# Eight-head attention: four heads scored together on 32-row tiles, with a second, transposed scoring in place of transposes

## The reference

```python
# L2; hidden is (2, 128, 16, 16), S = 256 places, HEADS = 8 of 16 channels
qk_hs = concat([hidden, embedding], axis=1)         # 128 + 64 channels; the embedding is constant
q, k, v = qk_hs @ Wq, qk_hs @ Wk, hidden @ Wv       # per place; split into 8 heads of 16
scores = einsum('bhqd,bhkd->bhqk', q, k) * 16 ** -0.5
attn = softmax(scores, axis=-1)
o = einsum('bhqk,bhkd->bhqd', attn, v)              # heads side by side: 128 channels
x3 = (o @ Wout + bout) + hidden                     # input of block L3
# L3 begins: f = chan_ln(x3) * g; q, k, v = dwconv3x3(conv1x1(f)); ...
```

## Time and profile before

| | |
|---|---|
| runs | 93.95, 95.25, 97.65 us; median 95.25 |
| profiled execution: span from the first to the last instruction | 94.5 us, 1637 instructions |
| what lies around the span | not recorded for that execution; median of the runs less the span is 0.75 us |
| granted TensorE clock | 1.000 over the span |
| busy: PE / weight loads / DVE / ACT / POOL | 84.6 / 61.4 / 67.1 / 53.2 / 30.9 us |
| DMA | 5.01 MB, 53 GB/s over the span |

### The profile page before, as it was taken

One profiled execution on the slowest core, in us unless ns is written; L12 is line 12 of the kernel. 1 busy time (PEld: TensorE's weight loads), 2 busy tenths in 40 slices (PEclk: granted clock), 3 DMA queues, 4 the chain that ended last, 5 costly groups with the idle time before them and its releaser, 6 DMA issues.

```text
span 94.5 us, 1637 instructions
## 1 busy us (share of the span) xinstructions
PE 84.6 (90%) x510; PEld 61.4 (65%) x510; DVE 67.1 (71%) x195; ACT 53.2 (56%) x168; POOL 30.9 (33%) x62
## 2 busy tenths in 40 slices
PE   4987999999999789899999999899999868979960
PEld 1333789756776569588776766678899635756540
DVE  1527456684677675997778699697999983877861
ACT  3200035924942504899989996996199454903830
POOL 7006199200000009910010003048876840235320
PEclk9999999999999999999999999999999999999999
DMA  1899100000000000772930000000000000000003
GB/s 52 228 363 390 44 0 0 0 0 7 0 0 3 0 0 0 237 210 68 285 98 0 0 0 0 0 7 0 0 0 3 0 0 10 0 0 3 0 0 111
DMA packets 5561, 5.01 MB, mean 53 GB/s; under 512 B 304, under 2 KB 5040, under 8 KB 5552
## 3 DMA queue, kind: packets, MB, share of 16 engines
q1 hardware_dynamic: 5264, 4.18, 13.4%
q10 hardware_dynamic: 288, 0.72, 2.6%
HBM read 3.59 MB, written 1.31 MB: 52 GB/s over the span
## 4 chain that ended last, share of the span: by engine, by line
PE 51%; DVE 19%; ACT 9%; issue 6%; POOL 6%; DMA 5%; SPq 0%; POOLq 0%; DVEq 0%; ACTq 0%
PE bank L886 7%; PE bank L1067 6%; DMA wa<-in_pack_a 5%; POOL vacc L277 3%; PE bank L1086 3%; ACT p L400 3%; DVE st L506 3%; PE bank L879 3%; PE bank L909 2%; DVE nmax L700 2%; PE bank L1004 2%; PE bank L926 2%; PE bank L981 2%; PE bank L1147 2%; PE bank L1034 2%
## 5 line engine op out<-in xcount | busy, mean ns | idle before, releaser
L367 ACT ACTIVATE p<-bank,nmax 128x256 f32<-128x256 f32 x32 | 14.9, 487 | 1.2 <-DVE nmax L700 0.9
L277 POOL TENSOR_TENSOR vacc<-vacc,p 128x240 f32<-128x240 f32 (+1 forms) x16 | 10.8, 675 | 6.8 <-ACT p L400 5.1
L886 PE MATMUL bank<-wa,p 128*128 128x128 f32 x80 | 12.5, 275 | 0.3 <-ACT pT L374 0.3
L700 DVE TENSOR_REDUCE nmax<-bank 128x2 f32<-128x512 f32 x16 | 10.7, 681 | 2.6 <-PE bank L1067 2.6
L236 POOL TENSOR_TENSOR rs<-ve,mhalf 128x2 f32<-128x2 f32 x8 | 5.6, 695 | 17.7 <-DVE ve L513 17.7
L894 PE MATMUL bank<-warm 128*128 128x512 bf16 x28 | 10.1, 495 | 1.2 <-DVE warm L519 1.2
L886 PEld LDWEIGHTS bank<-wa,p 128*128 128x128 f32 x80 | 9.3, 140 | 2.6 <-issue 0.9
L257 POOL TENSOR_SCALAR qh<-q,wb 128x256 f32<-128x256 f32 x8 | 4.5, 585 | 18.4 <-DVE q L687 18.4
L1147 PE MATMUL bank<-convw,fsh 128*128 128x128 f32 x72 | 9.0, 275 | 0.0
L1147 PEld LDWEIGHTS bank<-convw,fsh 128*128 128x128 f32 x72 | 8.7, 192 | 0.2
L1067 PE MATMUL bank<-k,qh 128*128 128x256 f32 x32 | 8.2, 383 | 0.4 <-ACT p L367 0.4
(11 more groups left out here) (205 smaller groups left out, 179.3 us busy)
## 6 DMA issues: line engine op xcount, KB each, us to landing
wc<-in_pack_c SPq DMA_DIRECT2D x1, 649.0 KB, 8.6
wb<-in_pack_b SPq DMA_DIRECT2D x1, 612.0 KB, 7.5
tapw<-in_taps ACTq DMA_DIRECT2D x1, 576.0 KB, 6.7
stack_q<-stacks_q SPq DMA_DIRECT2D x2, 256.0 KB, 3.2
stack_k<-stacks_k SPq DMA_DIRECT2D x2, 256.0 KB, 3.8
stacks_q<-parts_q SPq DMA_DIRECT2D x2, 192.0 KB, 2.1
stacks_k<-parts_k SPq DMA_DIRECT2D x2, 192.0 KB, 2.3
wa<-in_pack_a SPq DMA_DIRECT2D x1, 320.0 KB, 6.5
```

Source lines behind the costliest of these rows:

```text
L277: nc.gpsimd.tensor_add(vacc[b][:, oy, ox], vacc[b][:, oy, ox], vprod[n - 1][:, iy, ix]).then_inc(s["vsum_d"], 1)
L367: nc.scalar.activation(p2[u % P2_RING][:, t, :], tiles(bank[u % S2_BANKS])[:, t, :], ACT.Exp, bias=nmax2[b][:, h, t:t + 1], accum_out=sum2 ...
L700: nc.vector.tensor_reduce(nmax2[b][:, h, :], tiles(bank[u % S2_BANKS]), AX.X, ALU.max, negate=True).then_inc(s["max2_d"], 1)
L886: last = nc.tensor.transpose(tiles(dst)[:, i, t * 128:(t + 1) * 128], src[:, t, i * 128:(i + 1) * 128], ident)
```

## The change

Only block L2's attention changes, with the banks that L3 uses (`LA` to `LD`).

- `qm2` and `km2` replace q, k and `qh2`: two masked copies of q and of k for each batch, one for each group `g` of four heads. In a copy each head has its 16 channels in its own 32-row strip of partitions and the other 16 rows of the strip are zero; `km2` holds a one in one of these spare rows (`SHIFT_ROW`), by ACT's bias `kone`. DVE makes q's copies of batch 0, ACT all others. The masks come from three small reductions and one scaling on DVE (`half_masks`).
- `group_scores`: the four heads of a group are scored by matmuls with 32 rows each, on four row strips of the array, into four banks.
- DVE takes minus the maximum of each row into a column of `nmx2` (`group_max`), PE transposes that (`max_transposes`, two 128x128), and DVE adds it to `qm2`, so that the spare row of a head's strip holds minus the maximum (`shift_add`, giving `qa2`).
- `group_scores_T` scores a second time with the operands exchanged: the result is transposed and already shifted. ACT takes one exponential of 128x512 for a head (`head_exp`), straight to `pT2`. The transposes and their copies go, and so do the sums on ACT.
- `v2` is filled with ones, so that the mixing product also gives the sum of the probabilities in a spare row. `o2_norm` works on each group by itself: a 32x32 block transpose on DVE, a reciprocal, another such transpose, a multiplication. `woutm` is the output weight with each group's spare rows set to zero, and `w2_out` is two products.
- The embedding's products are accumulated in the banks of q and k, for each batch, just before `qk2`. The pieces, their copies and SP's ten DMAs go. Five `keep_clock` products among the heads go. `vprod` has memory of its own.

```diff
+            def half_masks(b):
+                dve.wait_ge(s["b_in"], 16)
+                nc.vector.tensor_reduce(kmask[:, :], B("headcol").rearrange("p (i g) -> p g i", g=NG), AX.X, ALU.add).then_inc(s["mask_d"], 1)
+                for g in range(NG):
+                    nc.vector.tensor_reduce(kone[:, g:g + 1], ident.rearrange("p (i r) -> p r i", r=QUAD)[:, SHIFT_ROW[g], :],
+                                            AX.X, ALU.add).then_inc(s["mask_d"], 1)
...
+            def k2_evac(b):
+                act.wait_ge(s["k2_p"], b + 1)
+                act.wait_ge(s["mask_d"], 2 + NG)
+                for g in range(NG):
+                    nc.scalar.activation(km2[b][:, g, :], bank[4 * b + 1][:, 0:N], ACT.Identity, bias=kone[:, g:g + 1],
+                                         scale=kmask[:, g:g + 1]).then_inc(s["k2_d"], 1)
+            def head_exp(u):
+                act.wait_ge(s["st2_p"], u + 1)
                 if u >= PT2_RING:
                     act.wait_ge(s["pv2_p"], (u - PT2_RING) // HG + 1)
-                nc.scalar.activation(pT2[u % PT2_RING][:, :, :], tiles(bank[4 + u % T2_BANKS]), ACT.Copy).then_inc(s["pT2o_d"], 1)
+                nc.scalar.activation(pT2[u % PT2_RING][:, :, :], tiles(bank[BANK2[u]]), ACT.Exp).then_inc(s["e2_d"], 1)
...
+            for stage, b in ((k2_evac, 0), (k2_evac, 1), (q2_evac, 1), (v2_evac, 0), (v2_evac, 1)):
+                stage(b)
+            for u in range(STEPS):
+                head_exp(u)
...
+            def group_max(grp):
+                b, g = divmod(grp, NG)
+                dve.wait_ge(s["nmx_zeroed"], NG)
+                if b:
+                    dve.wait_ge(s["nT2_p"], grp - NG + 1)
+                for i in range(HG):
+                    u = grp * HG + i
+                    dve.wait_ge(s["s2_p"], u + 1)
+                    col = QUAD * i + SHIFT_ROW[g]
+                    nc.vector.tensor_reduce(nmx2[g][:, :, col:col + 1], tiles(bank[BANK2[u]]), AX.X, ALU.max,
+                                            negate=True).then_inc(s["max2_d"], 1)
+            def shift_add(grp):
+                b, g = divmod(grp, NG)
+                dve.wait_ge(s["nT2_p"], grp + 1)
+                nc.vector.tensor_add(qa2[b][:, g, :], bank[BANK2[grp * HG + HG - 1]][:, 0:N], qm2[b][:, g, :]).then_inc(s["qa2_d"], 1)
+            def o2_norm(b, g):
+                dve.wait_ge(s["pv2_p"], NG * (b + 1) if b == 0 else NG * b + g + 1)
+                cols = slice(g * N, (g + 1) * N)
+                nc.vector.transpose(oT2[b][:, cols], mixed(b, g)).then_inc(s["vec"], 1)
...
+                nc.vector.reciprocal(rT2[b][:, g, :], sums).then_inc(s["vec"], 1)
...
+                nc.vector.transpose(rb2[b][:, g, :], rT2[b][:, g, :].unsqueeze(2).broadcast_to([128, N // QUAD, QUAD])).then_inc(s["vec"], 1)
...
+                nc.vector.tensor_mul(o2[b][:, g, :], mixed(b, g), rb2[b][:, g, :]).then_inc(s["o2_d"], 1)
...
-                             (ce_transpose, 0), (co_product, 0),
-                             (ce_transpose, 1), (co_product, 1), (qk2, 0), (v2_product, 0), (qk2, 1)):
+                             (ce_transpose, 0), (embedding(0), 0), (co_product, 0),
+                             (ce_transpose, 1), (embedding(1), 0), (co_product, 1), (embedding(0), 1), (embedding(1), 1), (qk2, 0)):
                 stage(b)
...
+            def group_scores(grp, heads):
+                b, g = divmod(grp, NG)
+                pe.wait_ge((s["q2_d"], s["q2b_d"])[b], g + 1)
+                pe.wait_ge(s["k2_d"], NG * b + g + 1)
+                for i in heads:
+                    if (w := before_in_bank(grp * HG + i)) is not None:
+                        pe.wait_ge(s["e2_d"], w + 1)
+                for t in range(NT):
+                    for i in heads:
+                        u = grp * HG + i
+                        rows = slice(QUAD * i, QUAD * (i + 1))
+                        product = nc.tensor.matmul(tiles(bank[BANK2[u]])[:, t, :], qm2[b][rows, g, t * 128:(t + 1) * 128], km2[b][rows, g, :],
+                                                   start=True, stop=True, tile_position=(QUAD * i, 0))
+                        if t == NT - 1:
+                            product.then_inc(s["s2_p"], 1)
...
+            group_scores(0, (0, 1, 2, 3))
+            qk2(1)
+            v2_product(0)
+            v2_product(1)
+            pe.wait_ge(s["q2b_d"], NG)
+            pe.wait_ge(s["v2_d"], NG * NB)
+            group_scores(1, (0, 1, 2, 3))
+            max_transposes(0)
+            group_scores_T(0)
+            group_scores(2, (0, 1))
+            max_transposes(1)
+            group_scores_T(1)
+            group_mix(0)
+            group_scores(2, (2, 3))
+            max_transposes(2)
+            group_scores_T(2)
+            group_mix(1)
+            group_scores(3, (0, 1))
+            group_scores(3, (2, 3))
+            w2_out(0)
+            max_transposes(3)
+            group_scores_T(3)
+            group_mix(2)
+            x3_transposes(0)
+            rb3_spread(0)
+            k_1x1(0)
+            group_mix(3)
+            v_1x1(0)
```

More of the change, by code:

```diff
@@ L17 @@
 TAPS = 9
-PARTS = 3
-PAIRS = C // D
+SHIFT_ROW = (D, 0)
 GN_GROUP = 4
@@ L983, in scores1, with embedding, stage @@
                 last.then_inc(s["s1_p"], 1)
-            def embedding(b):
-                for n, we in enumerate(("wqe", "wke")):
-                    last = nc.tensor.matmul(bank[5][:, n * N:(n + 1) * N], B(we)[0:EMB, :], B("emb")[0:EMB, :], start=True, stop=True)
-                last.then_inc(s["emb_p"], 1)
+            def embedding(n):
+                def stage(b):
+                    nc.tensor.matmul(bank[4 * b + n][:, 0:N], B(("wqe", "wke")[n])[0:EMB, :], B("emb")[0:EMB, :], start=True, stop=False)
+                return stage
             def p1_transposes(b):
```

297 lines of the change are left out of this document (100 added, 197 removed).

## The result

| | before | changed |
|---|---|---|
| median of the runs, us | 95.45 | 111.72 |
| lowest and highest | 93.95 to 97.65 (4 runs) | 110.48 to 113.94 (4 runs) |
| ratio, 95% interval | | 1.178 [1.171, 1.185] |
| span of the profiled execution | 94.5 | 108.7 |

Slower, as forecast, but by 16.3 us and not by 8.4: outside the range of 98.5 to 111. Both spans can be cut at three instructions that both kernels have, all on DVE: the first batch's `x2`, and the two `f_norm`. A run's time is 1.7 to 1.9 us above its span in every run for which both are known, but for one at 2.1 and one at 2.5.

The account below looks back on a forecast made before the run. The chain of dependent steps in the head stage bounds the kernel, not engine busy time. The second batch's statistics come 8.4 us later, carried in full to the end: 95.25 + 8.4 = 103.6 us; range 98.5 to 111.

Parts of the forecast that it names:

- rival (3): Head stage: TensorE's clock falls to 1.2 GHz for half the stage, +5.6 us, giving 109.2; chance 0.12.
- second scores of groups 0, 1 and 2: Head stage, scoring again with the maximum shifted in: 1.2 us for group 0, which ends at 43.95 us.
- Groups of scores: Head stage on PE: eight 32-row products on four row strips take 1.2 us to the last result.
- block transposes: The 32x32 transposes on DVE in the norms: 0.45 us each, with 0.3 and 0.8 as ends.
- four maxima: DVE's row maxima for one group of four heads: 2.45 us.
- Rivals (1): Scoring groups: weight loads not hidden, +0.76 us a group, +6.1 for eight, giving 109.7; chance 0.10.
- (2): Scoring groups: no row tiling at all, groups at 3.8 us and halves at 1.9, giving 120.6; chance 0.04.
- The way to `x2(0)`: Ahead of the heads: removing the embedding there gains 0.8 us, four mask instructions take 0.7; 0.4 of the gain left.
- the embedding's products: Ahead of the heads on PE: batch 1's two products delay `qk2(0)` by 0.86 us; batch 0's two cost nothing.
- DVE's idle time: Head stage: DVE has 15.6 us of own work in 24 us and waits some 8 us.
- what lies around the span: Whole run: the median of the runs lies 0.75 us above the profiled span, carried into the forecast time.
- rival (4): Head stage: not slower, groups overlap so well that DVE never waits; 95.3 us; chance 0.09.

Follow-up runs that it names:

- a_fill: The changed kernel with 53 products that nothing reads put into twelve waits of PE: 105.12 us, ratio 1.121 to the kernel before.

## Why the prediction was wrong

**What failed: rival (3), the clock.** The step is "Against it: from 68.10 to the end PE is busy 21.03 of 26.40, with waits too, at 1.00". From that stretch, busy to 80%, I judged one for which my own count was 14 of 25 us, and gave the fall 0.12 and half the stage. It was busy 6.91 of 12.06 ahead of the fall, and the clock was 0.50 for 13.65 of 39.06 us and for two shorter pieces of 3.4 us, one in the stage and one behind it. The sum held nothing for this. Price, from a_fill: 6.6 us of the time, and 7.0 behind `x2(0)` (5.9 in the stage, 1.1 after it). The rival's size, 5.6 for half the stage, was near; its chance was not.

**What held.** With the clock held (a_fill) the span is 103.0, forecast 102.9. That it is this close is luck: the stage from q's copy was 33.2 us and not 31.75, of which 0.4 were unread products in the way, and an early clock gave back 1.1 at its start. Step by step, second scores of groups 0, 1 and 2 ended 9.0, 14.4 and 20.7 us after q's first copy; forecast 8.65, 13.9 and 19.6. `f_norm(0)` 67.38 (67.05), the second batch's statistics 74.08 (74.0), `f_norm(1)` 76.57 (76.5). Groups of scores cost 1.15 (1.2), block transposes 0.45 (0.45), four maxima 2.5 (2.45). The tail moved unchanged: 26.4 us in before and changed alike. Rivals (1) and (2) are dead by the 1.15.

**Terms off in size.** The way to `x2(0)` gained 0.7 and not 0.4, the masks costing nothing there; the embedding's products put 1.5 between `x2(0)` and q's copy (1.31 before, 2.81 now) where I had 0.86; moving them gave back 1.26 there, 0.99 in the stage. DVE's idle time from the first maximum to `x3_sum(0)` was 10.3 us in a_fill, not 8. And what lies around the span is 1.8 us, not 0.75: I had compared one execution with the median of others whose early part was shorter. On the forecast span it would have given 104.7 us and not 103.6, with no meaning for the kernel.

**Not slower, rival (4)**, asked for DVE never waiting; it waited 21.7 of 39.06 us. That the banks speak against it agrees with the traces: with the clock held, DVE still waited 2.85 us for scores that needed banks of the group ahead, and in the best order found a cycle of four heads took about 6 us. No run with more free banks tests it alone.

Why the change is slow: before, each head's maximum, exponentials, transposes and copies overlapped with other heads', and three engines were over 80% busy. The change takes off much of that work, but it makes second scores wait for a maximum that has to go through DVE, PE and DVE again, four heads at a time with eight banks. Work fell, the chain grew, and PE became so thin that its clock fell too. The clock and the detour are shown by the runs that took them away; which part of the detour is the dear one is argued from the waits alone.

## What to carry to other kernels

When a change removes work from an engine that was full, ask what the clock of TensorE will be afterwards: take the share of its busy time that your own new chain implies, and compare it with a stretch of rows that is as thin, not with a fuller one; no run here gives the share from which the clock falls. Test it by filling the waits with unread products, all of them: a kernel that gets faster by more PE work had lost its clock. Price a detour (here the maximum's way into the second scores) by leaving it out once, since order alone could win back 1.4 of its 15 us. And cut the span at instructions that both kernels have, because an early part of varying length hides a gain of under 2 us in the medians.
